# The first of three attention layers rewritten: 32-row score tiles, rows moved by DMA, and a step's projections, turns and output rows at its end

## The chip, the cores and the metric

The kernel runs on one core of one Trainium2 chip. The metric is the device time of one execution in microseconds (us). Three runs of the kernel before gave a median of 1830.98 us (1827.04 to 1831.57). The engines are named as in the profile: PE is TensorE, DVE is VectorE, ACT is ScalarE, POOL is GpSimd, SP is SyncE, which here only issues DMAs.

## The reference

Eight sequences of 256 rows and 160 channels pass through a small cross-attention layer, then through a transformer block of self-attention, cross-attention and a gated feed-forward. All of it is in FP32. Only the first layer is touched:

```python
residual = x                                   # (8, 256, 160)
text, ip = ctx[:, :77], ctx[:, 77:]            # of 512 context rows, 256 channels
q = split_heads(x @ Wq.T, 20)                  # 20 heads of 8 channels
out_text = attend(q, text @ Wk.T,   text @ Wv.T,   1 / sqrt(8))
out_ip   = attend(q, ip @ Wk_ip.T,  ip @ Wv_ip.T,  1 / sqrt(8))
x = (out_text + out_ip) @ Wo.T + bo + residual
# then, untouched: x += self_attention(norm(x)); x += cross_attention(norm(x), ctx); x += gated_ff(norm(x))
```

Each head has two softmaxes over the same queries, one over the 77 text keys and one over the 435 others, with a maximum and a sum of its own.

## The kernel before

Each layer is a function with a program for each engine, written out by hand; semaphores tie them together. FP32 precision on PE's fast FP32R format comes from splitting an operand into a high part (its rounded value) and a low part (the rest) and adding the products high x high, high x low and low x high.

`narrow_attention_layer` is the first layer. Its unit is a step, one group of 4 heads of one batch: 5 groups times 8 batches make 40 steps. A group's 4 heads take 32 rows each of the 128 partitions. These 32 rows are the head's 8 channels four times over: the weights are given with every column repeated four times, so that the projections themselves (`project`, L1281) put the channels on all four places. Marks by row (`q_signed`, `q4`, `k_signed`, `k4`; L1422, L1423, L1427, L1507 to L1521) then leave the high or the low part on each place, and the matmul over 32 rows adds the split products up. `masked_q` (L1409) writes a copy of q for each head, with the other heads' rows zero, so that a score matmul runs over all 128 rows and yields one head's scores.

A step has five stages that run in neighbouring steps, so that PE has work of several groups at hand: projections of group t; scores of t-1 (`score`, L1262), one head and 128 queries at a time into a double-buffered tile, whose negated maxima over text and other keys DVE takes (`maximum`, L1485); the maxima are turned by a transpose (L1363) and ACT places them as two extra rows of the masked q (L1439); turned scores of t-2, keys down and queries across (`turned_scores`, L1274), which then come out with the maximum already taken off, and which ACT exponentiates (`exp`, L1402); weighted sums of t-3 (L1322), where v has extra columns of ones, so that the denominators come out as rows of the same result; and for t-4 the `pick` matmul (L1356), which repeats the denominators on the rows of the sums, two reciprocals (L1494) and a product (L1532). In each group of five steps stand V's projection (L1376) and the output rows (L1345, added to x at L1516).

PE's order inside a step is written in `step`: eight slots, each with a score, a part of the projections or of the weighted sums, and turned scores. Ten steps, two batches, make a turn; of the four turns the first and the last are written out, and a hardware loop runs the middle two. SP loads the weights, then x and ctx of each batch, single-buffered. POOL does nothing in the loop.

## Time and profile before

| | us |
|---|---|
| median of 3 runs | 1830.98 |
| the profiled execution | 1826.65 |
| its span | 1824.9 |
| PE busy in the span | 1669.2 (91%) |
| DVE busy | 1163.7 (64%) |
| ACT busy | 951.1 (52%) |
| POOL busy | 346.0 (19%) |
| granted TensorE clock, mean | 0.971 |

The busy times are those of all four layers. The first layer runs from the start to about 533 us. The matmuls are pipelined, and their ends are modelled, so where PE is back to back the distance between two starts is what an instruction costs, not its duration. The granted clock is a share of 2.4 GHz; it has two levels, 1.2 and 2.4 GHz, and a value between them is a mean over a stretch.

### The profile page before, as it was taken

The numbers are of one execution on the slowest core, as the hardware profiler recorded it, in microseconds if no ns is written. First come the engines' busy times: TensorE is split into PE (matmuls) and PEld (weight loads), VectorE is DVE, ScalarE is ACT, GpSimd is POOL, SyncE is SP. The second block draws the span as 40 slices with busy tenths as digits, with TensorE's granted clock in tenths as the row PEclk, the third lists the DMA queues.
The fourth block names the chain that finished last, engine by engine and source line by source line (L and its number), as shares of the span: only waits on it lengthen the run. The fifth ranks groups of instructions, "written<-read, shape, count | busy, mean of one in ns | idle before, by whom it ended". The sixth has DMA issues, their size and how long they took to land. (4 is left out here: it accounts for less than half of the span.)

```text
span 1824.9 us, 43431 instructions
## 1 busy us (share of the span) xinstructions
PE 1669.2 (91%) x18560; PEld 1334.9 (73%) x18560; DVE 1163.7 (64%) x1934; ACT 951.1 (52%) x1634; POOL 346.0 (19%) x254
## 2 busy tenths in 40 slices
PE   5999989999967999999975999999999999999768
PEld 3677666667636888888864787878888887878558
DVE  5777767887757677677644565656565656554366
ACT  5778767887754444555424544444444444443233
POOL 1000000000003222222211332323232323222200
PEclk9999989999978999999997999999999999999979
DMA  5000000000002000000002000000101010000010
GB/s 214 18 19 1 18 20 1 18 19 1 1 23 80 2 2 2 2 2 2 2 1 68 25 2 25 1 25 2 24 2 25 2 25 2 1 2 2 2 45 22
DMA packets 13675, 34.21 MB, mean 19 GB/s; under 512 B 2033, under 2 KB 5105, under 8 KB 13105
## 3 DMA queue, kind: packets, MB, share of 16 engines
q1 hardware_dynamic: 13488, 31.47, 5.5%
q8 instruction: 149, 2.44, 0.6%
q14 instruction: 38, 0.30, 0.1%
HBM read 30.15 MB, written 1.31 MB: 17 GB/s over the span
## 5 line engine op out<-in xcount | busy, mean ns | idle before, releaser
L1485 DVE TENSOR_REDUCE l_negmax<-l_pscore 128x1 f32<-128x77 f32 (+1 forms) x640 | 233.2, 413 | 74.1 <-PE l_pscore L1262 69.5
L1046 DVE TENSOR_REDUCE a_negmax<-a_pscore 128x2 f32<-128x1024 f32 x160 | 195.6, 1223 | 115.5 <-PE a_pscore L821 115.5
L973 ACT ACTIVATE raw_weights<-a_pst 128x1024 f32<-128x1024 f32 x160 | 164.0, 1025 | 162.3 <-PE a_pst L846 161.6
L1402 ACT ACTIVATE l_probs<-l_pst 128x512 f32<-128x512 f32 x320 | 184.4, 598 | 75.1 <-PE l_pst L1274 74.2
L1119 POOL TENSOR_TENSOR raw_weights<-raw_weights 128x512 f32<-128x512 f32 x80 | 106.7, 1337 | 342.5 <-ACT raw_weights L973 342.5
L1262 PE MATMUL l_pscore<-l_k,l_qm 128*128 128x512 f32 x320 | 147.2, 460 | 11.5 <-DVE l_negmax L1485 6.0
L692 POOL TENSOR_TENSOR a_key_sum<-a_probs 128x1024 f32<-128x1024 f32 x40 | 96.2, 2405 | 240.8 <-ACT a_probs L568 240.8
L870 PE MATMUL a_pj<-a_ct,a_wk 64*128 64x512 f32 x960 | 130.3, 403 | 4.8 <-DVE a_ql L1034 3.8
L1274 PE MATMUL l_pst<-l_qm,l_k 128*128 128x256 f32 x640 | 131.0, 287 | 4.0 <-ACT l_probs L1402 3.3
L625 DVE TENSOR_REDUCE a_negmax<-a_pscore 128x4 f32<-128x1024 f32 x80 | 97.7, 1221 | 57.9 <-PE a_pscore L445 57.9
L880 PE MATMUL a_pj<-a_wv,a_ct 128*128 128x256 f32 x960 | 128.6, 291 | 4.1 <-DVE a_kl L1034 4.1
L1274 PEld LDWEIGHTS l_pst<-l_qm,l_k 128*128 128x128 f32 x640 | 116.0, 192 | 21.9 <-issue 5.0
L880 PEld LDWEIGHTS a_pj<-a_wv,a_ct 128*128 128x128 f32 x960 | 121.3, 194 | 4.8 <-issue 3.9
L1119 POOL TENSOR_TENSOR a_key_sum<-raw_weights 128x512 f32<-128x512 f32 x80 | 102.6, 1285 | 100.9 <-ACT raw_weights L973 100.9
L1060 DVE RECIPROCAL a_recip<-a_pv 128x256 f32<-128x256 f32 x40 | 70.3, 1758 | 78.7 <-PE a_pv L903 78.7
L870 PEld LDWEIGHTS a_pj<-a_ct,a_wk 64*128 64x128 f32 x960 | 87.5, 187 | 26.0 <-DVE a_ql L1034 7.8
L1322 PE MATMUL l_pv<-l_probs,l_v 128*32 128x256 f32 x1280 | 102.7, 394 | 0.5 <-ACT l_sums L1445 0.5
L256 POOL MEMSET a_ln_half<- 128x2 f32 x2 | 0.2, 100 | 542.9 <-POOLq L1158 528.1
L637 DVE RECIPROCAL a_recip<-a_pv 128x256 f32<-128x256 f32 x40 | 70.3, 1757 | 49.5 <-PE a_pv L508 49.5
L568 ACT ACTIVATE a_probs<-a_pst 128x1024 f32<-128x1024 f32 x80 | 81.9, 1023 | 37.8 <-PE a_pst L468 37.8
L840 PE MATMUL a_pst<-a_qh,a_kh 64*128 64x256 f32 x640 | 95.5, 292 | 6.3 <-ACT raw_weights L973 5.6
L1262 PEld LDWEIGHTS l_pscore<-l_k,l_qm 128*128 128x128 f32 x320 | 60.8, 190 | 48.1 <-issue 38.9
(186 smaller groups left out, 3840.5 us busy)
## 6 DMA issues: line engine op xcount, KB each, us to landing
l_ct<-in_ctx_t SPq DMA_DIRECT2D x8, 512.0 KB, 3.7
a_ct<-in_ctx_t SPq DMA_DIRECT2D x8, 512.0 KB, 5.0
a_ct<-in_ctx_t SPq DMA_DIRECT2D x16, 256.0 KB, 5.8
l_x<-in_x_t SPq DMA_DIRECT2D x8, 256.0 KB, 2.7
raw_weights<-in_a_wq SPq DMA_DIRECT2D x2, 960.0 KB, 4.9
raw_weights<-in_a_wv SPq DMA_DIRECT2D x1, 1920.0 KB, 11.3
a_wo<-in_a_wo SPq DMA_DIRECT2D x2, 800.0 KB, 6.4
xs<-in_x SPq DMA_DIRECT2D x8, 160.0 KB, 4.0
```

The source lines that it names most:

```text
L625: nc.vector.tensor_reduce(to, pscore[:].rearrange("p h (q k) -> p h q k", q=QT), AX.X, ALU.max, negate=True).then_inc(max_done, 1)
L692: nc.gpsimd.tensor_tensor(key_sum[:, e % 2], probs[:, e % 2, :, 0, :], probs[:, e % 2, :, 1, :], ALU.add).then_inc(sum_ready, 1)
L870: last = mm(pj[:, t, :], wk[OWN[t], hw, s, u * P:(u + 1) * P], cts[b % 2][OWN[t], hc, s, :], start=k == 0, stop=k == len(C_ROWS) - 1)
L880: last = mm(pj[:, kt // 2, (kt % 2) * STEP_COLS:(kt % 2 + 1) * STEP_COLS], cts[b % 2][:, hc, 2 * s, kt * P:(kt + 1) * P], wv[:, hw, s, u * ...
L973: nc.scalar.activation(probs[:, 2 * i:2 * i + 2, 2 * n:2 * n + 2, :], pst[:].rearrange("p h (k q) -> p h k q", k=2), ACT.Exp, scale=SCALE) ...
L1046: nc.vector.tensor_reduce(to, pscore[:], AX.X, ALU.max, negate=True).then_inc(max_done, 1)
L1119: nc.gpsimd.tensor_tensor(key_sums[n][:, two], probs[:, two, 2 * n, :], probs[:, two, 2 * n + 1, :], ALU.add).then_inc(sum_ready, 1)
L1262: mm(pscore[:, i % 2, :], qm[:, buf, j, qt * P:(qt + 1) * P], k4[:, buf, :], start=True, stop=True).then_inc(score_ready, 1)
L1274: last = mm(pst[:, n % 2, i * SQ:(i + 1) * SQ], k4[:, buf, kt * P:(kt + 1) * P], qm[:, buf, j, :], start=True, stop=True)
L1322: last = mm(pv[j * ROWS:(j + 1) * ROWS, 0:SQ], v[:, vb, kt, GROUP * u3 + j, :], probs[:, par, j, kt, :], start=kt == 0, stop=kt == KT - 1)
L1402: nc.scalar.activation(probs[:, par, j, 2 * kb:2 * kb + 2, :], pst[:, n % 2, :].rearrange("p (k q) -> p k q", k=2), ACT.Exp, scale=SCALE). ...
L1485: last = nc.vector.tensor_reduce(negmax[:, par, qt, j, s:s + 1], pscore[:, i % 2, keys], AX.X, ALU.max, negate=True)
```

## The change

The first layer is written anew. The other layers, and the reference's arithmetic, are the same.

The projections are made once per batch for all heads, with plain weights: ip keys and text keys of 16 heads (128 columns), `rest` (the last 4 heads' keys of both kinds), q, and v in four key blocks. ACT copies each result twice (`take`), once rounded (hi) and once in full, and POOL subtracts (`low`). SP then moves rows by DMA (`stack`): for each group, channel c of a head's high or low part goes to row 4c + r of a stack of 128 rows, so that a head has 32 rows again: three places for the split products and a fourth for the maxima, against marks of ones among the keys. POOL rounds the stacks (`round_stack`).

Scores and turned scores use 32 rows per head, two heads at once on different row groups of the array, instead of masked copies of q over 128 rows. One score tile holds two heads and 128 queries and isn't double-buffered; DVE reduces two heads at once. The maxima come back by one addition on DVE (`place_max`). The denominators of a batch are moved by DMA to 40 rows, inverted at once (`invert`), and spread over the sums' rows by five matmuls per batch (`spread`). There is one PSUM bank for projections and turned maxima (`pj`) and one for sums, spread denominators and output rows (`px`). V's copies leave POOL's zeros where nothing stands.

In a step PE now has four slots, each with one score pair and its turned scores, the weighted sums in the first; everything else stands behind them: a projection, the turned maxima, a piece of finishing (`s0`, `s1`, `s2` or `out`), another projection. `PLAN` says which. The projections are for the next batch, so the program begins with five steps that have nothing else. There is no hardware loop; every step is written out.

```diff
-    TURNS = B // 2
+    T_LAG, V_LAG = 2, 3
     SCALE = float(D0) ** -0.5
-    total = GROUPS * B
-    WIDE = GROUPS * P
+    ALL = GROUPS * B
+    FIRST, LAST = -GROUPS, ALL + 8
+    K_ROLES, Q_ROLES = ("hi", "lo", "hi"), ("hi", "hi", "lo")
+    MOVES = [16 * (6 if u < GROUPS - 1 else 9) for u in range(GROUPS)]
...
+        PLAN = {0: ("ip", "text"), 1: ("rest", "q"), 2: (None, None), 3: ("v0", "v1"), 4: ("v2", "v3")}
+        def finished(t):
+            b, k = divmod(t - 2 * GROUPS + 1, GROUPS)
+            return (("s0", "s1", "s2", "out")[k], b) if k < 4 and 0 <= b < B else None
...
+            def stack(m, u):
+                sp.wait_ge(k_low if u < GROUPS - 1 else rest_low, m + 1)
+                sp.wait_ge(q_low, m + 1)
+                wait(sp, rounded, GROUPS * (m - 1) + u + 1)
+                main = u < GROUPS - 1
+                rows = slice(u * ROWS, (u + 1) * ROWS) if main else slice(0, ROWS)
...
+                    for keys, src in moves:
+                        sp.dma_start(k_stack[r:P:4, u, keys], src.bitcast(FP32)).then_inc(stacked[u], 16)
+                for r, half in enumerate(Q_ROLES):
+                    sp.dma_start(q_stack[r:P:4, u, :], q_n[half][rows, 0 if main else 1].bitcast(FP32)).then_inc(
+                        stacked[u], 16)
...
+                if u == 2 and b + 1 < B:
+                    for group in range(GROUPS):
+                        stack(b + 1, group)
...
+            def score(g, s):
+                m, u = divmod(g, GROUPS)
+                qt, pair = s // 2, s % 2
+                if s == 0:
+                    pe.wait_ge(rounded, g + 1)
+                wait(pe, max_done, 4 * g + s)
+                for h in range(2):
+                    rows = slice((2 * pair + h) * ROWS, (2 * pair + h + 1) * ROWS)
+                    last = mm(pscore[:, h, :], q4[rows, u, qt * P:(qt + 1) * P], k4[rows, u, :],
+                              start=True, stop=True)
+                last.then_inc(score_ready, 1)
...
+            def turned_scores(g, s):
+                m, u = divmod(g, GROUPS)
+                n, pair = s // 2, s % 2
+                if s == 0:
+                    pe.wait_ge(pj_read, pj_uses["turn", g] + 1)
+                wait(pe, exp_done, 4 * g + s - 1)
                 for i in range(2):
+                    kt = 2 * n + i
+                    for h in range(2):
+                        rows = slice((2 * pair + h) * ROWS, (2 * pair + h + 1) * ROWS)
+                        last = mm(psts[s % 2][:, h, i * SQ:(i + 1) * SQ], k4[rows, u, kt * P:(kt + 1) * P],
+                                  q4[rows, u, :], start=True, stop=True)
                 last.then_inc(st_ready, 1)
...
+            def project(what, m):
+                wait(pe, pj_read, pj_uses[what, m])
...
+                elif what in ("ip", "text", "rest"):
+                    cols, n = {"ip": (IP, SK), "text": (TXT, TEXT + 1), "rest": (RST, SK)}[what]
+                    for k, (hw, hc, s) in enumerate(C_TERMS):
+                        last = mm(pj[:, 0:n], wc[:, hw, s, cols], ct[:, hc, s, 0:n],
+                                  start=k == 0, stop=k == len(C_TERMS) - 1)
...
+            def weighted_sums(g):
+                m, u = divmod(g, GROUPS)
+                wait(pe, px_read, px_uses["sum", g])
+                pe.wait_ge(pj_read, pj_uses["v3", m] + 1)
+                pe.wait_ge(exp_done, 4 * (g + 1))
+                for kt in range(KT):
+                    for j in range(GROUP):
+                        last = mm(px[j * ROWS:(j + 1) * ROWS, 0:SQ], v[:, m % 2, kt, GROUP * u + j, :],
+                                  probs[:, g % 2, j, kt, :], start=kt == 0, stop=kt == KT - 1)
+                last.then_inc(px_ready, 1)
+            def turn_max(g):
+                wait(pe, pj_read, pj_uses["turn", g])
+                pe.wait_ge(max_done, 4 * g + 4)
+                if g == 0:
+                    pe.wait_ge(*first_in)
+                for qt in range(QT):
+                    last = nc.tensor.transpose(pj[:, qt * P:(qt + 1) * P], negmax[:, g % 2, qt, :], ident)
+                last.then_inc(pj_ready, 1)
...
+            def finish(what, b):
+                wait(pe, px_read, px_uses[what, b])
+                if what == "out":
+                    pe.wait_ge(px_read, px_uses["s2", b] + 1)
...
+                else:
+                    pe.wait_ge(recip_done, b + 1)
+                    if b == 0:
+                        pe.wait_ge(small_in, 64)
+                    k = int(what[1])
+                    for i, u in enumerate(range(2 * k, min(2 * k + 2, GROUPS))):
+                        last = mm(px[:, i * SQ:(i + 1) * SQ], spread[:, u, :], recip[:], start=True, stop=True)
+                last.then_inc(px_ready, 1)
...
+            def step(t):
+                for s in range(4):
+                    if here(t):
+                        score(t, s)
+                    if here(t - T_LAG):
+                        turned_scores(t - T_LAG, s)
+                    if s == 0 and here(t - V_LAG):
+                        weighted_sums(t - V_LAG)
+                if projected(t, 0):
+                    project(*projected(t, 0))
+                if here(t - 1):
+                    turn_max(t - 1)
+                if finished(t):
+                    finish(*finished(t))
+                if projected(t, 1):
+                    project(*projected(t, 1))
...
+            def take(what, m):
+                act.wait_ge(pj_ready, pj_uses[what, m] + 1)
...
+                if what[0] != "v":
+                    for hi, x, src in pairs:
+                        copy(hi, src)
+                        copy(x.bitcast(FP32), src).then_inc(pj_read, 1)
...
+            def maximum(g, s):
+                qt, pair = s // 2, s % 2
+                if s == 0 and g >= 2:
+                    dve.wait_ge(pj_ready, pj_uses["turn", g - 2] + 1)
+                dve.wait_ge(score_ready, 4 * g + s + 1)
+                to = negmax[:, g % 2, qt].rearrange("p (j d r) -> p j d r", d=D0, r=4)[:, 2 * pair:2 * pair + 2, :, 3]
+                for k, keys in enumerate((slice(0, TEXT), slice(TEXT, SK))):
+                    last = nc.vector.tensor_reduce(to[:, :, k], pscore[:, :, keys], AX.X, ALU.max, negate=True)
                 last.then_inc(max_done, 1)
...
+            def place_max(g):
+                dve.wait_ge(pj_ready, pj_uses["turn", g] + 1)
+                to = q4[:, g % GROUPS, :]
+                nc.vector.tensor_tensor(to, to.bitcast(FP32), pj[:, 0:SQ], ALU.add).then_inc(pj_read, 1)
+            def invert(b):
+                dve.wait_ge(den_in[b % 2], 16 * GROUPS * (b // 2 + 1))
+                if b:
+                    dve.wait_ge(px_ready, px_uses["s2", b - 1] + 1)
+                n = GROUPS * DENS
+                nc.vector.reciprocal(recip[0:n, :], den[:, b % 2, :]).then_inc(recip_done, 1)
...
+            def round_stack(g):
+                m, u = divmod(g, GROUPS)
+                if g == 0:
+                    pool.wait_ge(marks_placed, 16 * GROUPS)
+                pool.wait_ge(stacked[u], MOVES[u] * (m + 1))
+                wait(pool, st_ready, 4 * (g - GROUPS + 1))
+                nc.gpsimd.tensor_copy(k4[:, u, :], k_stack[:, u, :])
+                nc.gpsimd.tensor_copy(q4[:, u, :], q_stack[:, u, :]).then_inc(rounded, 1)
```

PE's order in a whole step of the steady part: first before (`l_pa`, `l_pb` hold projections, `l_pv` the sums; this is from the turned maxima to the middle of the ip projection of a step).

```order
L1363 MATMUL l_pb<-identity,l_negmax 128x128 x2
L1262 MATMUL l_pscore<-l_k,l_qm 128x512
L1281 MATMUL l_pa<-l_nt,l_wq 128x256 x4
L1274 MATMUL l_pst<-l_qm,l_k 128x256 x2
L1262 MATMUL l_pscore<-l_k,l_qm 128x512
L1281 MATMUL l_pa<-l_ct,l_wk 128x256 x6
L1274 MATMUL l_pst<-l_qm,l_k 128x256 x2
L1262 MATMUL l_pscore<-l_k,l_qm 128x512
L1281 MATMUL l_pb<-l_ct,l_wk_ip 128x512 x3
L1274 MATMUL l_pst<-l_qm,l_k 128x256 x2
L1262 MATMUL l_pscore<-l_k,l_qm 128x512
L1281 MATMUL l_pb<-l_ct,l_wk_ip 128x512 x3
```

Now, a whole step with u = 0 and the start of its end block (`l_px` holds the sums, `l_pj` the projection, then the turned maxima, `l_recip`<-`l_spread` the spread denominators).

```order
L1304 MATMUL l_pscore<-l_k,l_q 128x512 x2
L1319 MATMUL l_pst<-l_q,l_k 128x256 x4
L1356 MATMUL l_px<-l_probs,l_v 32x256 x16
L1304 MATMUL l_pscore<-l_k,l_q 128x512 x2
L1319 MATMUL l_pst<-l_q,l_k 128x256 x4
L1304 MATMUL l_pscore<-l_k,l_q 128x512 x2
L1319 MATMUL l_pst<-l_q,l_k 128x256 x4
L1304 MATMUL l_pscore<-l_k,l_q 128x512 x2
L1319 MATMUL l_pst<-l_q,l_k 128x256 x4
L1338 MATMUL l_pj<-l_ct,l_wc 128x512 x6
L1367 MATMUL l_pj<-identity,l_negmax 128x128 x2
L1385 MATMUL l_px<-l_recip,l_spread 128x256 x2
```

Projections stood between scores and gave DVE time for its maxima; now only turned scores do, and the weighted sums once, and the projection and the turned maxima stand behind the last score.

ACT's order over most of a step, before (`l_qm` is the masked q):

```order
L1402 ACTIVATE l_probs<-l_pst 128x512 x2
L1422 ACTIVATE l_q_signed<-l_pa,l_marks 128x256
L1423 ACTIVATE l_k_signed<-l_pa,l_marks 128x77
L1402 ACTIVATE l_probs<-l_pst 128x512 x2
L1427 ACTIVATE l_k_signed<-l_pb,l_marks 128x435
L1409 ACTIVATE l_qm<-l_q,l_marks 128x256 x2
L1402 ACTIVATE l_probs<-l_pst 128x512
L1409 ACTIVATE l_qm<-l_q,l_marks 128x256 x2
L1402 ACTIVATE l_probs<-l_pst 128x512 x3
L1439 ACTIVATE l_qm<-l_pb 2x256 x4
```

and now, over a step with u = 0 (`l_k_hi`, `l_k_lo` are the two copies of a projection):

```order
L1426 ACTIVATE l_probs<-l_pst 128x2x512
L1412 ACTIVATE l_sums<-l_px 128x256
L1426 ACTIVATE l_probs<-l_pst 128x2x512 x3
L1412 ACTIVATE l_k_hi<-l_pj 128x435
L1412 ACTIVATE l_k_lo<-l_pj 128x435
L1412 ACTIVATE l_k_hi<-l_pj 128x77
L1412 ACTIVATE l_k_lo<-l_pj 128x77
L1426 ACTIVATE l_probs<-l_pst 128x2x512
L1412 ACTIVATE l_sums<-l_px 128x256
L1426 ACTIVATE l_probs<-l_pst 128x2x512 x3
```

The copies of q per head and the placing of maxima are gone, and the exps are half as many and twice as long; the projection's copies stand behind the last exp of the step, and the turned maxima on PE wait for them.

## Rows read from the trace of the kernel before

**Rows 1.** stage table, first layer; its first row names the columns

```profile
core 0: us, PE busy (x) PEld busy (x) DVE busy (x) ACT busy (x) POOL busy (x), PEclk, DMA share, GB/s
23.57:509.88 486.31, 453.76 (x3268) 331.15 (x3268) 373.95 (x909) 374.01 (x849) 0.00 (x0) 0.98 0.04 15
509.88:533.70 23.82, 16.85 (x108) 10.30 (x108) 8.71 (x13) 7.13 (x16) 0.00 (x0) 0.79 0.00 0
```

**Rows 2.** groups by line, first layer (count, busy us, mean ns)

```profile
L1485 DVE TENSOR_REDUCE l_negmax<-l_pscore 128x1 f32<-128x435 f32 x320 | 191.8, 599 | 0.0
L1402 ACT ACTIVATE l_probs<-l_pst 128x512 f32<-128x512 f32 x320 | 184.4, 598 | 75.1 <-PE l_pst L1274 74.2
...
L1485 DVE TENSOR_REDUCE l_negmax<-l_pscore 128x1 f32<-128x77 f32 x320 | 72.7, 227 | 74.1 <-PE l_pscore L1262 69.5 <-issue 4.2
L1409 ACT ACTIVATE l_qm<-l_q,l_marks 128x256 fp32r<-128x256 f32 x160 | 71.9, 504 | 0.0
...
L1439 ACT ACTIVATE l_qm<-l_pb 2x256 fp32r<-2x256 f32 x160 | 60.0, 375 | 26.4 <-PE l_pb L1363 23.4
```

**Rows 3.** timeline of PE, first layer: start, duration, instruction

```profile
46.48 1.04 PE L1376 MATMUL l_pb<-l_wv,l_ct 128*128 128x320 f32 x6
...
48.97 0.85 PE L1281 MATMUL l_pa<-l_ct,l_wk 128*128 128x256 f32 x6
...
50.12 0.86 PE L1281 MATMUL l_pb<-l_ct,l_wk_ip 128*128 128x512 f32 x3
50.82 0.40 PE L1274 MATMUL l_pst<-l_qm,l_k 128*128 128x256 f32 x2
...
53.68 0.40 PE L1274 MATMUL l_pst<-l_qm,l_k 128*128 128x256 f32 x2
54.01 0.64 PE L1322 MATMUL l_pv<-l_probs,l_v 128*32 128x256 f32 x8
54.58 0.49 PE L1262 MATMUL l_pscore<-l_k,l_qm 128*128 128x512 f32 x1
```

**Rows 4.** timeline of PE and DVE, third layer, tight score chain

```profile
1302.00 0.28 PE L840 MATMUL a_pst<-a_qh,a_kh 64*128 64x256 f32 x2
...
1302.12 0.29 PE L842 MATMUL a_pst<-a_qh,a_kl 64*128 64x256 f32 x2
...
1316.18 1.21 DVE L1046 TENSOR_REDUCE a_negmax<-a_pscore 128x2 f32<-128x1024 f32 x1
...
1317.44 0.50 PE L821 MATMUL a_pscore<-a_kh,a_qh 64*128 64x512 f32 x2 [0.51 <-DVE a_negmax L1046]
...
1317.99 1.23 DVE L1046 TENSOR_REDUCE a_negmax<-a_pscore 128x2 f32<-128x1024 f32 x1 [0.60 <-PE a_pscore L821]
```

**Rows 5.** groups by line and shape, whole run

```profile
L973 ACT ACTIVATE raw_weights<-a_pst 128x1024 f32<-128x1024 f32 x160 | 164.0, 1025 | 162.3 <-PE a_pst L846 161.6
...
L1532 DVE TENSOR_TENSOR l_ot<-l_sums,l_recip 128x256 f32<-128x256 f32 x40 | 17.0, 425 | 1.4
```

**Rows 6.** timeline of PE: the same output rows at either clock

```profile
492.04 2.88 PE L1345 MATMUL l_pd<-l_wo,l_ot 128*128 128x160 f32 x20
...
528.44 4.40 PE L1345 MATMUL l_pd<-l_wo,l_ot 128*128 128x160 f32 x20 [2.39 <-DVE l_ot L1532]
```

**Rows 7.** timeline of PE where the loop body starts again

```profile
255.00 0.79 PE L1262 MATMUL l_pscore<-l_k,l_qm 128*128 128x512 f32 x1 [3.57 <-issue]
```

**Rows 8.** stage table, PE alone: us, busy (x), clock, DMA share, GB/s

```profile
510.00:515.00 5.00, 2.75 (x12) 0.78 0.00 0
1712.00:1714.00 2.00, 0.88 (x16) 1.00 0.00 0
```

**Rows 9.** timeline of SP's queue and POOL at the start

```profile
1.20 4.40 POOL L1557 MEMSET l_v<- 128x2560 f32 x2
...
2.62 0.90 SPq L80 DMA_DIRECT2D raw_weights<-in_l_wk  x2
```

**Rows 10.** DMA issues by line: KB each, median us from issue to landing

```profile
l_x<-in_x_t SPq DMA_DIRECT2D x8, 256.0 KB, 2.7
```

More of the change, by code:

```diff
@@ new lines, in finished @@
+        def finished(t):
+            b, k = divmod(t - 2 * GROUPS + 1, GROUPS)
+            return (("s0", "s1", "s2", "out")[k], b) if k < 4 and 0 <= b < B else None
+        pj_uses, px_uses = {}, {}
+        for t in range(FIRST, LAST):
+            for use in (projected(t, 0), ("turn", t - 1) if here(t - 1) else None, projected(t, 1)):
+                if use:
+                    pj_uses[use] = len(pj_uses)
+            for use in (("sum", t - V_LAG) if here(t - V_LAG) else None, finished(t)):
+                if use:
+                    px_uses[use] = len(px_uses)
@@ L1461, in _, with copy, high_inputs @@
-            for part in range(3):
-                hi_inputs(0, part)
-            weights.high(act, pieces)
+            def copy(out, x, **kw):
+                return nc.scalar.activation(out, x, ACT.Copy, **kw)
+            def high_inputs(m):
+                act.wait_ge(ctx_in, 16 * (m + 1))
+                copy(cts[m % 2][:, 0], ct32[:]).then_inc(in_hi, 1)
+                act.wait_ge(x_in, 16 * (m + 1))
+                copy(nts[m % 2][:, 0], x32[:, 0])
+                copy(nts[m % 2][0:EXT, 2], x32[0:EXT, 1]).then_inc(in_hi, 1)
@@ new lines, in step @@
+            def step(t):
+                b, u = divmod(t, GROUPS)
+                for s in range(4):
+                    if here(t - T_LAG):
+                        exp(t - T_LAG, s)
+                    if s == 0 and here(t - V_LAG):
+                        copy_sums(t - V_LAG)
+                for place in range(2):
+                    if projected(t, place):
+                        take(*projected(t, place))
+                if u == 4 and b + 2 < B:
+                    high_inputs(b + 2)
@@ L1464, in _ @@
+            high_inputs(0)
+            act.wait_ge(wc_in, 16)
+            copy(wc[:, 0], raw_c).then_inc(w_hi, 1)
+            act.wait_ge(wq_in, 16)
+            copy(wq[:, 0], raw_q[:, 0])
+            copy(wq[0:EXT, 2], raw_q[0:EXT, 1]).then_inc(w_hi, 1)
             act.wait_ge(small_in, 64)
             act.wait_ge(v_marked, 1)
-            turns(act, step, 6)
+            for t in range(FIRST, LAST):
+                if t == -1:
+                    act.wait_ge(w_done, 3)
+                    load_next(act)
+                step(t)
@@ new lines, in step @@
+            def step(t):
+                b, u = divmod(t - 2 * GROUPS + 2, GROUPS)
+                for s in range(4):
+                    if here(t):
+                        maximum(t, s)
+                    if s == 1 and t >= 0 and t % GROUPS == 0 and t // GROUPS + 1 < B:
+                        low_rest(t // GROUPS + 1)
+                if here(t - 1):
+                    place_max(t - 1)
+                if finished(t):
+                    take(*finished(t))
+                if u == 0 and 0 <= b < B:
+                    invert(b)
@@ new lines, in _ @@
+            low_inputs(0)
+            for i in range(2):
+                nc.gpsimd.memset(v[:, i], 0.0)
+            nc.gpsimd.memset(negmax[:], 0.0)
+            nc.gpsimd.memset(recip[:], 0.0).then_inc(zeroed, 1)
+            for t in range(FIRST, LAST):
+                b, u = divmod(t, GROUPS)
+                for place in range(2):
+                    if projected(t, place) and projected(t, place)[0] in ("text", "rest", "q"):
+                        low(*projected(t, place))
+                if FIRST + 2 <= t < ALL - 3:
+                    round_stack(t + 3)
+                if u == 4 and b + 2 < B:
+                    low_inputs(b + 2)
+                if u == 0 and 0 <= b < B:
+                    if b == 0:
+                        pool.wait_ge(*first_in)
+                        pool.wait_ge(small_in, 64)
+                    nc.gpsimd.tensor_tensor(xs[:, b], xs[:, b], bo_rows[:], ALU.add).then_inc(biased, 1)
@@ new lines, in laid_out @@
+    wo = np.zeros((GROUPS, GROUP, 2, ROWS // 2, C), np.float32)
+    for u in range(GROUPS):
+        for s in range(2 * GROUP):
+            spread[2 * GROUP * u + s, u, s, 1:1 + D0] = 1
+    for k in range(2):
+        wo[:, :, k, 1:1 + D0] = w0["Wo"].reshape(GROUPS, GROUP, D0, C)
+    layers = {"l0": {"wq": wq, "wc": halves(wc).transpose(1, 0, 2), "wo": wo.reshape(GROUPS, P, C).transpose(1, 0, 2),
+                     "bo_rows": rows(inputs["L0_xattn_bo"]), "marks": marks,
+                     "spread": spread.reshape(P, GROUPS, P), "key_marks": key_marks.reshape(ROWS, SK)}}
```

541 lines of the change are left out of this document (200 added, 341 removed).

## The prediction

> **What bounds the kernel now.** I read the stage table first, then the groups by line, then the timelines. The first layer's scores begin at 23.57 and end at 509.88 us [rows 1]: 486.3 us for 40 steps, 12.2 us each, with PE busy 453.8 of them at a granted clock of 0.98. DVE is busy 374.0 and ACT 374.0, about 9.4 us a step each. So PE sets the step, with DVE and ACT close behind. The tail takes 23.8 us more at clock 0.79 [rows 1]. Inside one step PE goes back to back: three 512-column projections take 0.70 us from their start to that of the next instruction (50.12 to 50.82), six of 256 columns take 0.68 (48.97 to 49.65, where the six end their issue and their last one drains), two 256-column turned scores about 0.24, and one key block of the weighted sums with its two changes of tile shape 0.57 (54.01 to 54.58) [rows 3]. The rest of the program (two more attention layers and the feed-forward) isn't touched; it should move as a block.
>
> **What is computed less.** Of PE's work in a step, the 8 score matmuls of 512 columns and the 16 of 256 become 8 and 16 on 32 rows, issued in pairs on different row groups. The nearest rows are the pairs on 64 rows of the third layer: two matmuls of 256 columns start every 0.12 us (1302.00 to 1302.12) [rows 4]. So a pair of 512 costs 0.24, and a step's scores and turned scores cost 4 x 0.24 + 4 x 0.24 = 1.9 us instead of 8 x 0.24 + 8 x 0.24 = 3.8. That 32-row pairs go as 64-row pairs do is assumed: no row shows a 32-row tile. If they went one after the other, a step would have 1.9 us more. The projections are made once per batch for 20 heads, not once per group of four with every column repeated: per batch 12 matmuls of 512 columns, 8 of 256, 6 of 78, 6 of 320 and 18 of 160, by rows 3 about 2.8 + 0.9 + 0.5 + 0.9 + 1.5 = 6.6 us, against 5 x (0.45 + 0.68 + 1.40) + 3.5 = 16.2 before. DVE's 16 maxima of 599 and 227 ns (6.6 us) become 8 over two heads: the two sizes give 1.04 ns an element, so 154 elements take 0.31, 870 take 1.05, and the pair 1.29 (the 1024 elements of L1046 take 1.21 to 1.23, [rows 4]). ACT's four masked copies (504 ns) and four placements (375 ns) [rows 2] go; the eight exps of 598 ns become four of 1025 [rows 5]. The reciprocals fall to one per batch.
>
> **What is added: waits in a row.** The score tile isn't double-buffered any more: score s waits for maximum s-1. The third layer has this same chain: the reduce ends at 1317.39 (1316.18 + 1.21), the matmul starts at 1317.44, the next reduce at 1317.99, so DVE idles 0.60 in each turn [rows 4]. One turn costs 0.60 + 1.29 = 1.89 us. In a step: score 0, turned 0 and the weighted sums, now together, 0.24 + 0.24 + 0.1 + 4 x 0.45 + 0.15 = 2.5 (a key block of 0.57 without its changes of shape is about 0.45, which I take; with them the sum would be 2.9), which hides maximum 0; then two turns of 1.89; then score 3 and turned 3, 0.6. Together 6.9 us.
>
> Behind it stands the block at the step's end, all of it through one PSUM bank, pj, whose next use waits for its reader. ACT's last exp ends about 1.3 us into the block (turned 3 ready at about 0.25, 1.03 more). The five kinds of step:
> - u = 0: ip projection 1.5 until ready, two copies of 435 (under the 598 ns of 512 [rows 2]) 0.95, turn 0.2, the spread matmuls 0.9 beside DVE's addition of the turned maxima (0.43 [rows 5], 1.0 with both handshakes), text 0.45: 4.1
> - u = 1: rest 1.5, copies 1.1, turn and addition 1.0, q 0.85: 4.45
> - u = 2: turn 0.2, output rows 20 at 0.136 (2.88 in all [rows 6]): 3.05
> - u = 3: v0 1.04 [rows 3], its copies until 2.1, turn and addition 1.0, v1 0.5: 3.6
> - u = 4: v2 0.9, its copy at 1.65, turn and spread 1.2, v3 0.5: 3.35
> They sum to 18.55. A batch costs 5 x 6.9 + 18.55 + 0.9 (low_rest on DVE between two maxima, the output row's addition ahead of the next maximum) = 54.0 us, a step 10.8; 40 steps 432. The first steps lack turned scores, sums and output rows (-7), the last five have no next batch to project (-10, since the score chain then sets them): 415.
>
> **Start and end.** Before, the first score stands at 23.57. Now ACT takes its first projection only once v is marked, which waits for POOL's memsets of v (4.40 for two, [rows 9]) behind its low parts of the first inputs: about 15 us. Four projections follow one by one with their copies, partly at the slow clock, about 2.5 us each (25), POOL's low part 1.3, six DMAs at 0.45 of issue [rows 9], about 2 of landing (2.7 for 256 KB [rows 10]), two roundings 1.6: first score at 32.7, 9 us later. After the last score's step come two steps of turned scores bound by exps (11), the sums (2), then denominators by DMA, reciprocal, three spreads and the output rows, about 17: 30 us against 23.8. The unrolled program loses the loop's restart, where PE waited 3.57 us for its instructions [rows 7]; that is within the old 486.3. POOL's roundings, the moved rows (33 DMAs a batch at 0.45 = 15 us of SP's time in 54) and the one DMA of denominators per step lie beside this with three steps of slack, and cost nothing unless the slack is used up.
> Sum at full clock: 32.7 + 415 + 30 = 478 against 533.7, a gain of 55 us.
>
> **The clock is the unknown.** PE was busy 93% of the steps before. Now, in the middle of each step, it is busy for about 0.6 us in every 1.89, and the block at the end has idle spans of 1 us. In the rows, a stretch with PE busy 0.88 of 2.00 us kept 1.00, one with 2.75 of 5 fell to 0.78, which is a part of it at 1.2 GHz instead of 2.4 [rows 8]. The new middle lies under both. What a fall costs: 20 output matmuls take 2.88 us at 2.4 GHz and 4.40 when most of them run at 1.2 [rows 6]. A step wholly at 1.2 GHz would pay its sums and its end block almost twice and each score a little, 2.3 + 0.9 + 2.15 = 5.4 us. Bounds: 0 (clock kept) and 40 x 5.4 = 215 us. I expect that the dense parts (sums, projections) bring it back each time, and take a fifth of the time as slow, between the row that kept its clock and the one that fell (0.78 means 0.44 of its time slow): 1.1 us a step, 43 us. So 478 + 43 = 521, 12 us less than before. The profiled execution took 1826.65 us (span 1824.9) and the median is 1830.98; the difference carries over, so 1831 - 12 = 1819.
>
> The Trainium skill, "TensorE: Matmul & The Clock Gate", section "A second HAM failure mode: psum-queue depth-cycling", tells of a kernel whose short idles between groups of matmuls make the clock swing between its two levels, so that it pays for each fall and each rise. By it the second rival below would be the case. The trace agrees as far as it goes: 0.98 in the dense steps and 0.79 in the tail [rows 1].
>
> **Rivals.**
> - The clock holds. For: 0.88 of 2.00 busy kept 1.00 [rows 8], and no idle span here is above 1.4 us. Against: the new middle is thinner. Time: 1831 - 55 = 1776.
> - The clock falls in nearly every step and needs its dense part to rise, so that 40% of the first layer is slow: 0.4 x 215 = 86, less 55: 1862, slower. The place is the weighted sums and the ip, rest and output matmuls that follow the thin middle; it decides from a slow share of a quarter (54 us) upwards.
> - The moved rows come late: a step waits for the roundings because SP issues 33 DMAs in a row behind the denominators. The slack of three steps (32 us) covers 15 us of issue plus 3; it would need an issue of over 0.9 us each. Then 8 times some 8 us: about 1883 with the forecast's clock.
> - The pairs on 32 rows don't overlap: 40 x 1.0 on the path (half of 1.9 lies beside the maxima): 1859.
>
> **How the numbers follow.** Forecast 0.45, clock holds 0.17, clock falls often 0.30, late rows 0.04, no overlap 0.04. What a measurement of this kernel can't tell from no change is 0.3%, 5.5 us. The forecast's own range is 1797 to 1840 (slow shares from a tenth to three tenths), of which two thirds lie under 1825.5 and a quarter above 1836.5. That gives faster 0.47, same 0.13, slower 0.40. The range for 8 in 10 is 1776 to 1862: it takes in the clock that holds, and reaches to the middle of the case where it falls often.
>
> **What would show it.** Right: first score near 33 us; DVE idle 0.6 before maxima 1 to 3; the score group's reduces near 1.05 and 0.31; steps of 11 to 12.5 us; the first layer ending near 521; granted clock 0.9 in it; the layers after it unchanged within 2 us. Wrong: a clock of 1.00 or under 0.85 in the steps, PE waiting for POOL's rounding, pairs of score matmuls 0.2 us apart, or a later layer that moves.

## The result, and the profile after

The changed kernel takes 1932.3 us (median of 4 runs, 1925.48 to 1938.95) against 1831.11 for the kernel before on the same chip: a ratio of 1.0558, 95% interval 1.0513 to 1.0602. The forecast was 1819 and the range ended at 1862, so it was wrong in its sign and outside its range. The profiled execution took 1938.95 us (span 1937.2), the longest of the four. Ratios in this document leave out executions more than 1.5% above the fastest of the same kernel; that concerns one run, with 9 extra matmuls.

The stage table of the changed kernel, with the columns of [rows 1]: the 40 steps, the tail of the first layer, then the other three layers.

```profile
36.30:603.00 566.70, 436.13 (x2721) 289.56 (x2722) 249.09 (x396) 213.80 (x298) 91.19 (x121) 0.66 0.12 34
603.00:640.20 37.20, 27.97 (x191) 18.08 (x190) 7.42 (x12) 9.49 (x12) 0.00 (x1) 0.75 0.01 2
640.20:1096.40 456.20, 402.21 (x5640) 338.98 (x5640) 303.33 (x351) 215.27 (x294) 120.01 (x64) 0.94 0.06 19
1096.40:1873.60 777.20, 740.86 (x9084) 599.63 (x9084) 423.60 (x498) 323.71 (x413) 216.74 (x177) 0.98 0.04 12
1873.60:1937.20 63.60, 57.25 (x444) 55.35 (x444) 45.51 (x145) 20.96 (x47) 4.15 (x6) 1.00 0.06 21
```

The first layer now ends at 640.20 instead of 533.70: 106.5 us of the 112.3 by which the span grew. DVE fell from 374.0 to 249.1 us of work and ACT from 374.0 to 213.8, as meant, but PE's 454 only to 436, although it has much less to do: the granted clock of the steps went from 0.98 [rows 1] to 0.66. A clock of 0.66 means that 2 x (1 - 0.66) = 0.68 of the time ran at 1.2 GHz.

The groups by line, of the changed kernel's whole run, that answer to [rows 2]:

```profile
L1304 PE MATMUL l_pscore<-l_k,l_q 32*128 32x512 f32 x320 | 102.9, 639 | 97.9 <-DVE l_negmax L1512 95.7 <-POOL l_q L1608 2.2
L1356 PE MATMUL l_px<-l_probs,l_v 128*32 128x256 f32 x1280 | 119.5, 539 | 1.3 <-ACT l_probs L1426 0.8 <-DVE l_ot L1542 0.4
```

and, for the 40 steps alone, DVE's maxima and ACT's exps:

```profile
L1512 DVE TENSOR_REDUCE l_negmax<-l_pscore 128x2 f32<-128x870 f32 x160 | 168.8, 1055 | 0.1
L1512 DVE TENSOR_REDUCE l_negmax<-l_pscore 128x2 f32<-128x154 f32 x160 | 51.1, 319 | 220.3 <-PE l_pscore L1304 219.7
L1426 ACT ACTIVATE l_probs<-l_pst 128x1024 f32<-128x1024 f32 x152 | 155.6, 1024 | 144.1 <-PE l_pst L1319 143.5
```

Every engine waits for another one: PE 96 us for DVE's maxima, DVE 220 us for PE's scores. PE waits for POOL's rounding of the stacks 2.2 us in all, so the moved rows are not late.

PE in one step of the changed kernel (start, duration, instruction), a step with v2 and v3, wholly at 1.2 GHz:

```profile
458.49 0.79 PE L1304 MATMUL l_pscore<-l_k,l_q 32*128 32x512 f32 x2
459.08 0.62 PE L1319 MATMUL l_pst<-l_q,l_k 32*128 32x256 f32 x4
459.64 3.64 PE L1356 MATMUL l_px<-l_probs,l_v 128*32 128x256 f32 x32
463.21 0.79 PE L1304 MATMUL l_pscore<-l_k,l_q 32*128 32x512 f32 x2
...
465.39 0.80 PE L1304 MATMUL l_pscore<-l_k,l_q 32*128 32x512 f32 x2 [0.96 <-DVE l_negmax L1512]
...
467.57 0.80 PE L1304 MATMUL l_pscore<-l_k,l_q 32*128 32x512 f32 x2 [0.96 <-DVE l_negmax L1512]
468.17 0.63 PE L1319 MATMUL l_pst<-l_q,l_k 32*128 32x256 f32 x4
468.73 1.57 PE L1344 MATMUL l_pj<-l_wc,l_ct 128*128 128x160 f32 x6
470.71 0.69 PE L1367 MATMUL l_pj<-identity,l_negmax 128*128 128x128 f32 x2 [0.42 <-ACT l_v L1412]
471.19 1.91 PE L1385 MATMUL l_px<-l_recip,l_spread 128*128 128x256 f32 x4
472.55 1.76 PE L1344 MATMUL l_pj<-l_wc,l_ct 128*128 128x160 f32 x6
474.24 0.79 PE L1304 MATMUL l_pscore<-l_k,l_q 32*128 32x512 f32 x2
```

The step takes 15.75 us. From score 0 to score 1, with the weighted sums between, are 4.72 us (458.49 to 463.21), and a turn is 2.18 (465.39 to 467.57). At 2.4 GHz a turn is 1.89, as forecast; the same lines earlier in the run:

```profile
380.67 0.50 PE L1304 MATMUL l_pscore<-l_k,l_q 32*128 32x512 f32 x2 [1.15 <-DVE l_negmax L1512]
381.01 0.39 PE L1319 MATMUL l_pst<-l_q,l_k 32*128 32x256 f32 x4
382.56 0.70 PE L1304 MATMUL l_pscore<-l_k,l_q 32*128 32x512 f32 x2 [1.16 <-DVE l_negmax L1512]
```

Where the clock falls can be read from the score pairs, which take 0.50 us at 2.4 GHz and 0.79 at 1.2. The next step of that stretch:

```profile
390.23 3.24 PE L1356 MATMUL l_px<-l_probs,l_v 128*32 128x256 f32 x32
393.39 0.50 PE L1304 MATMUL l_pscore<-l_k,l_q 32*128 32x512 f32 x2
...
395.28 0.50 PE L1304 MATMUL l_pscore<-l_k,l_q 32*128 32x512 f32 x2 [1.14 <-DVE l_negmax L1512]
...
397.16 0.79 PE L1304 MATMUL l_pscore<-l_k,l_q 32*128 32x512 f32 x2 [1.15 <-DVE l_negmax L1512]
...
398.31 1.57 PE L1344 MATMUL l_pj<-l_wc,l_ct 128*128 128x160 f32 x6
```

In 33 of the 40 steps the fourth score pair takes over 0.6 us, in 27 the first, but in only 13 and 8 the second and the third. So the weighted sums mostly do bring the clock back, but begin slow themselves; it then serves the thin middle, is gone again by the fourth score, and the block at the end runs at 1.2 GHz.

PE and POOL at the start of the changed kernel:

```profile
32.52 1.57 PE L1344 MATMUL l_pj<-l_wc,l_ct 128*128 128x160 f32 x6 [0.42 <-ACT l_v L1412]
36.30 0.79 PE L1304 MATMUL l_pscore<-l_k,l_q 32*128 32x512 f32 x2 [2.22 <-POOL l_q L1608]
...
48.77 2.90 PE L1338 MATMUL l_pj<-l_ct,l_wc 128*128 128x512 f32 x6 [5.13 <-POOL l_nt L1581]
...
53.51 0.50 PE L1304 MATMUL l_pscore<-l_k,l_q 32*128 32x512 f32 x2
```

```profile
35.30 0.61 POOL L1607 CAST l_k<-l_k_stack 128x512 fp32r<-128x512 f32 x1 [8.21 <-DMA l_q_stack<-l_q_lo]
...
43.44 0.61 POOL L1607 CAST l_k<-l_k_stack 128x512 fp32r<-128x512 f32 x1 [7.19 <-DMA l_q_stack<-l_q_lo]
...
45.60 2.34 POOL L1581 TENSOR_TENSOR l_ct<-l_ct 128x1024 fp32r<-128x1024 f32 x1
```

Step 0 takes 17.2 us, since POOL splits batch 1's inputs only behind roundings that wait for DMAs.

### The profile page after: what moved, and what is told of

It is laid out like the page before. It is cut to its first block and busy times, and to the rows that moved or that the text cites. A ratio compares the mean times of both kernels' runs of the same rounds, so it can differ in the third digit from the quotient of the medians.

```text
span 1937.2 us, 41189 instructions
## 1 busy us (share of the span) xinstructions
PE 1680.5 (87%) x18128; PEld 1314.0 (68%) x18128; DVE 1034.2 (53%) x1409; ACT 794.9 (41%) x1085; POOL 446.5 (23%) x384
## 5 line engine op out<-in xcount | busy, mean ns | idle before, releaser
L1512 DVE TENSOR_REDUCE l_negmax<-l_pscore 128x2 f32<-128x154 f32 x320 | 206.5, 687 | 220.5 <-PE l_pscore L1304 219.7
L1426 ACT ACTIVATE l_probs<-l_pst 128x1024 f32<-128x1024 f32 x160 | 163.3, 1024 | 146.7 <-PE l_pst L1319 146.1
L1304 PE MATMUL l_pscore<-l_k,l_q 32*128 32x512 f32 x320 | 102.9, 639 | 97.9 <-DVE l_negmax L1512 95.7
L1304 PEld LDWEIGHTS l_pscore<-l_k,l_q 32*128 32x128 f32 x320 | 37.5, 231 | 147.4 <-DVE l_negmax L1512 114.2
L1356 PE MATMUL l_px<-l_probs,l_v 128*32 128x256 f32 x1280 | 119.5, 539 | 1.3 <-ACT l_probs L1426 0.8
L844 PE MATMUL a_pst<-a_ql,a_kh 64*128 64x256 f32 x640 | 92.0, 282 | 0.0
L846 PE MATMUL a_pst<-a_neg_t,a_sel 64*128 64x256 f32 x640 | 92.0, 282 | 0.0
L842 PE MATMUL a_pst<-a_qh,a_kl 64*128 64x256 f32 x640 | 91.7, 281 | 0.0
```

The source lines that it names most:

```text
L1304: last = mm(pscore[:, h, :], q4[rows, u, qt * P:(qt + 1) * P], k4[rows, u, :], start=True, stop=True)
L1356: last = mm(px[j * ROWS:(j + 1) * ROWS, 0:SQ], v[:, m % 2, kt, GROUP * u + j, :], probs[:, g % 2, j, kt, :], start=kt == 0, stop=kt == KT - 1)
L1426: nc.scalar.activation(probs[:, g % 2, 2 * pair:2 * pair + 2, 2 * n:2 * n + 2, :], psts[s % 2][:].rearrange("p h (k q) -> p h k q", k=2), ...
L1512: last = nc.vector.tensor_reduce(to[:, :, k], pscore[:, :, keys], AX.X, ALU.max, negate=True)
```

## The experiments

Theory: the change's own sum at full clock is right, and the slow clock is the loss. Rival: the serial chain (single score tile, one bank, everything at the step's end) is the loss, and the clock only accompanies it. All ratios are to the kernel before, whose own is 1.

**Work added to PE beside the maxima.** Runs with 6 and with 2 extra matmuls in slots 1 to 3, 6 on 32 rows, and 6 on 32 columns:

```diff
+            def fill():
+
+                for i in range(6):
+                    mm(px[:, SQ:SQ + 256], wc[0:128, 0, 0, 0:P], wc[0:128, 0, 0, 0:256], start=True, stop=True)
+
...
+                    if s in (1, 2, 3) and here(t):
+                        if here(t - V_LAG):
+                            pe.wait_ge(px_read, px_uses["sum", t - V_LAG] + 1)
+                        fill()
```

The run with 2 has `range(2)`, the one on 32 rows `wc[0:32, ...]` in both operands, the one on 32 columns `px[0:ROWS, ...]` and `wc[..., 0:ROWS]`.

> The changed kernel with 6 extra matmuls of 128 rows and 256 columns (fp32r) behind the turned scores of slots 1, 2 and 3 of each step, into the unused half of the bank of the sums; their result is not used. They add 3 x 0.64 us of PE work a step at full clock, and nothing to the chain while it stands at full clock. Theory (the slow clock is the loss: 0.69 of the 40 steps' time was at 1.2 GHz, and a step wholly slow pays about 5.4 us): the granted clock of the first layer rises above 0.9, steps come to 10.5 to 11.5 us, the first layer ends near 500 instead of 640, time 1785 to 1820. Rival (the serial chain, maxima and one bank for projections, is the loss, and the low clock only accompanies the idle time): steps stay at 14 us or get longer, time 1930 or more.

> The same with 2 extra matmuls in each of slots 1 to 3, a third of the amount (0.64 us a step at full clock). Theory (slow clock is the loss): the slow share falls from 0.69 but not to nothing, and the time follows it at 5.4 us for a step wholly slow: between 1800 and 1920, on a line with the changed kernel and the run with 6. Rival (serial chain): 1930 to 1945.

> As the run with 6, but each extra matmul uses 32 rows of the array instead of 128, for the same time on PE. If the clock goes by the time in which PE streams, this gives what the run with 128 rows gives (within 15 us). If it goes by how many rows of the array work (the score pairs on 32 rows would then count little), the clock stays near 0.65 in the first layer and the time stays above 1900.

> As the run with 6 extra matmuls of 128 rows, but each uses only 32 of the array's columns (output rows) instead of 128; time on PE and rows of the array are as there. If the clock goes by the rows that work, time as with 128 x 128: 1820 to 1840. If it goes by rows times columns, this is as thin as the run on 32 rows: 1885 to 1910. If neither counts but the time alone, the run on 32 rows has no explanation.

| extra work | us | ratio, 95% | clock of the steps |
|---|---|---|---|
| none | 1932.3 | 1.0558 [1.0513, 1.0602] | 0.66 |
| 6, 128 rows x 128 columns | 1827.8 | 0.9983 [0.9973, 0.9992] | 0.97 |
| 2, 128 x 128 | 1895.1 | 1.0373 [1.0324, 1.0422] | 0.74 |
| 6, 32 rows x 128 columns | 1897.8 | 1.0365 [1.0341, 1.0389] | 0.73 |
| 6, 128 rows x 32 columns | 1823.7 | 0.9964 [0.9951, 0.9976] | 0.97 |

Adding useless work wins 104 us. The stage rows of the steps in these four runs, first with 6 of 128 x 128:

```profile
36.27:500.00 463.73, 407.85 (x3444) 296.88 (x3444) 250.12 (x397) 213.83 (x298) 91.39 (x121) 0.97 0.14 41
```

With 2 of 128 x 128:

```profile
33.37:561.00 527.63, 435.31 (x2960) 297.32 (x2961) 249.82 (x396) 213.47 (x298) 91.20 (x121) 0.74 0.13 36
```

With 6 of 32 rows x 128 columns:

```profile
34.43:568.00 533.57, 466.22 (x3441) 339.53 (x3442) 249.79 (x396) 213.36 (x298) 91.17 (x121) 0.73 0.12 36
```

With 6 of 128 rows x 32 columns:

```profile
36.34:498.00 461.66, 399.27 (x3448) 274.68 (x3448) 250.43 (x398) 213.32 (x298) 91.35 (x121) 0.97 0.14 42
```

Stage rows of the run with 6 of 128 x 128, five steps (one batch) and the step of the kind that was shown slow above:

```profile
222.14:280.08 57.94, 51.46 (x462) 38.12 (x462) 32.14 (x52) 28.83 (x41) 12.42 (x16) 1.00 0.14 41
269.20:280.08 10.88, 9.97 (x94) 7.53 (x94) 6.73 (x11) 5.15 (x7) 0.96 (x2) 1.00 0.09 23
```

That slow step in the changed kernel:

```profile
458.49:474.24 15.75, 13.41 (x76) 9.08 (x76) 6.38 (x11) 5.14 (x7) 0.96 (x2) 0.50 0.03 8
```

The extra work of the last slot stands on the path. A later run that has none there (9 in slots 1 and 2) has the same steps at 11.60, 11.98 and 10.11 us instead of 12.21, 12.62 and 10.81, so it costs 0.65. Without it a batch takes 57.94 - 5 x 0.65 = 54.7, where the forecast had 54.0. And the slow step pays 15.75 - (10.88 - 0.65) = 5.5 us, where the forecast had 5.4. The 0.65 is measured on three kinds of step and taken for all five. At 1827.8 us the run with 6 missed its own range of 1785 to 1820 by 8 us, far from the rival's 1930: the 0.65 in each of 40 steps, 26 us, was reckoned as nothing. So the theory stands for the gap between forecast and result, and the rival falls for it; what the block at the end costs at full clock was in the forecast, and is measured below. The run with 2 lies between, as expected.

The extra work on 32 rows came out between what its two theories gave (not within 15 us of the first run, not quite above 1900), but far nearer to "rows count": PE is busy 0.87 of the steps in it (466.22 of 533.57) and 0.88 in the run with 128 rows, yet the clock is 0.73 and 0.97; 32 columns with all rows hold 0.97. PE's time is not quite equal, though: in slot 3 the extra matmuls on 32 rows start beside the score pair on other rows (at 201.67 and 201.65), and at full clock PE then idles 0.34 and 0.45 us before scores 2 and 3, where the run with 128 rows has 0.25. That this little time makes the difference is unlikely beside the run with 2: PE is busy only 0.83 of the steps there, and the clock is the same (0.74). PE's timeline of the run on 32 rows shows it streaming when the clock falls: gaps of 0.3 us at most, and then a score pair of 0.79 us instead of 0.50:

```profile
224.73 0.97 PE L1391 MATMUL l_px<-l_wc 32*128 32x256 f32 x6
225.99 0.50 PE L1304 MATMUL l_pscore<-l_k,l_q 32*128 32x512 f32 x2 [0.29 <-DVE l_negmax L1521]
226.32 0.40 PE L1319 MATMUL l_pst<-l_q,l_k 32*128 32x256 f32 x4
226.56 1.16 PE L1391 MATMUL l_px<-l_wc 32*128 32x256 f32 x6
227.87 0.79 PE L1304 MATMUL l_pscore<-l_k,l_q 32*128 32x512 f32 x2 [0.15 <-DVE l_negmax L1521]
```

So idle time is hardly all. That the changed kernel's own scores (pairs of 32 rows where 128 stood) let the clock fall in the same way follows from this by analogy; it wasn't tried on them alone.

**The start alone.** The next layer's weights are asked for in step 8 instead of -1, and batch 1's inputs split ahead of the roundings:

```diff
-                if t == -1:
+                if t == 8:
                     act.wait_ge(w_done, 3)
                     load_next(act)
...
-                if u == 4 and b + 2 < B:
+                if u == (2 if b < 0 else 4) and b + 2 < B:
                     high_inputs(b + 2)
...
+                if b < 0 and u == 2:
+                    low_inputs(1)
                 if FIRST + 2 <= t < ALL - 3:
                     round_stack(t + 3)
...
```

> The changed kernel with another start only: the next layer's three weight DMAs are issued in step 8 instead of step -1 (where they share the DMA engines with the first stacks of moved rows), and batch 1's inputs are split on ACT and POOL in step -3, ahead of the roundings, instead of behind them. In the changed kernel the last DMA of stack 0 was issued at 30.87 and its reader on POOL began at 35.30, that of stack 1 took 8 us, and PE waited 5.1 us for POOL in step 0. Theory (contention and POOL's order at the start cost about 10 us): first score at 33 to 34, step 0 at 11 to 13 us instead of 17.2, time 1918 to 1926. Rival (the moved rows are late because SP issues 33 DMAs at 0.6 us each): first score and step 0 within 1 us of before, time 1928 to 1938.

1918.5 us, 1.0501 [1.0473, 1.0528]. The first score is at 33.85, and step 0 takes 11.97 us instead of 17.2; its stage row in this run:

```profile
33.85:45.82 11.97, 6.76 (x21) 3.71 (x21) 5.58 (x9) 1.28 (x3) 1.92 (x4) 1.00 0.27 69
```

The first score may be chance: it stands at 33.37 to 36.34 us in the five other runs whose start was left alone. Step 0 is not: it takes 16.9 to 19.8 us in those, and 12.0 to 13.4 in all six with the new start. The median fell by 13.8 us, by the two ratios by about 10, and their intervals just overlap; what lies beyond step 0 is steps at another clock later (0.67 over the steps), as it also differs between executions (1914.32 to 1927.22). Of the two edits, that of the weights is seen in the DMAs: the stack's DMAs of 64 KB land in 2.1 us between 25 and 50 us here, where the changed kernel had 5.9. How much of step 0 each edit won was not taken apart.

**The end block spread over the slots.** This undoes one part of the change and adds no work (PE's part; the readers on ACT and DVE move with it):

```diff
                     if s == 0 and here(t - V_LAG):
                         weighted_sums(t - V_LAG)
-                if projected(t, 0):
+                    if s == 1 and projected(t, 0):
                         project(*projected(t, 0))
-                if here(t - 1):
+                    if s == 2 and here(t - 1):
                         turn_max(t - 1)
-                if finished(t):
+                    if s == 2 and finished(t):
                         finish(*finished(t))
-                if projected(t, 1):
+                    if s == 3 and projected(t, 1):
                         project(*projected(t, 1))
```

> Undoes one part of the change: the work that stands together at a step's end is spread over the slots (first projection behind slot 1, turned maxima and finishing behind slot 2, second projection behind slot 3; the readers on ACT and DVE in the same slots). No work is added. Theory (thin middle of the step lowers the clock, and the end block stands on the path): the matmuls of the end block fill PE's idle time beside the maxima; step 2.3 + 1.9 + 2.3 + 1.9 + 0.6 = 9.0 us at full clock, slow share under 0.3, first layer 430 to 480, time 1730 to 1790. Rival (ACT's and DVE's readers of the one bank, now between the exps and maxima, delay the chain as much as before): steps 12 to 14 us, time 1870 to 1930.

> The spread version with the same new start. In the spread version step 0 took 19.8 us. Theory (start costs 10 us there too): 1752 to 1762, first layer ending near 457 to 465. Rival (the clock, slow at the start in either case, takes it back): 1764 to 1770.

> The spread version with the new start and extra matmuls of 128 rows and 256 columns where a slot is thin: 2 ahead of a projection, 6 where a step has none, 3 ahead of the finishing matmuls (none with the output rows). Spread fast steps were 8.5 to 10.2 us, 9.2 on average, and 0.29 of the steps' time was slow. Theory (the rest of the loss is again the clock): slow share under 0.1, time 1725 to 1745. Rival (the extra work is on PE's path in the slots with projections): steps 0.3 to 0.6 us longer at full clock, time as without it or up to 10 us more.

Spread: 1768.5 us, 0.9655 [0.9634, 0.9676]. With the new start: 1753.5, 0.9581 [0.9565, 0.9597]. With extra matmuls in its thin slots: 1734.2, 0.9482 [0.9466, 0.9498]. The stage row of the steps, spread alone:

```profile
35.04:437.60 402.56, 329.85 (x2728) 217.52 (x2728) 244.72 (x397) 210.07 (x298) 91.31 (x121) 0.85 0.16 47
```

Spread with the new start:

```profile
34.36:429.00 394.64, 329.83 (x2729) 218.74 (x2728) 244.79 (x397) 210.19 (x299) 88.36 (x119) 0.87 0.18 53
```

Spread with the new start and extra matmuls:

```profile
31.01:407.00 375.99, 344.31 (x3083) 245.45 (x3082) 245.17 (x398) 212.69 (x299) 88.37 (x119) 0.96 0.19 55
```

One batch of the second of them at full clock takes 45.8 us, 8.9 less than 54.7; its stage row:

```profile
237.28:283.11 45.83, 38.97 (x372) 26.96 (x372) 31.37 (x52) 28.23 (x43) 12.41 (x16) 1.00 0.19 51
```

So the block at the end cost 1.8 us a step even at full clock, 71 us in 40. The steps of the spread version take 164 us less than the changed kernel's (402.6 for 566.7): the other 93, by subtraction, came with the clock, 0.66 to 0.85. The rival of the first of these runs falls. That of the third was right in one half, since its batch at full clock grew from 45.8 to 47.5, 0.33 us a step, and wrong in the other: the time went down by 19 us.

**The change's own order with the clock held.** New start, 9 extra matmuls in slots 1 and 2 only:

> The changed kernel in its own order (everything else at the step's end), with the new start and 9 extra matmuls of 128 rows in slots 1 and 2 only, where they lie beside a maximum and not on the path. This is the closest to the forecast's sum at full clock: 33 to the first score, 54.0 us a batch, tail 30, first layer 478. The run with 6 had 57.9 us a batch at full clock, of which 5 x 0.64 was its last slot's extra work. Theory (that sum is right and only the clock was mis-sized): fast batches 54 to 55.5 us, first layer ending at 490 to 505, time 1787 to 1802. Rival (the step's end block costs more than I reckoned, extra work apart): batches stay near 57, time 1812 or more.

1822.6 us is the median; but the four executions lie between 1798.87 us (mean clock 0.963) and 1834.2 (0.941). The ratio is 0.9865 [0.9815, 0.9915]. In the profiled execution (1834.2) the clock still fell in most steps with v2 and v3. The other four steps of a batch in it, as a stage row:

```profile
405.49:450.49 45.00, 41.39 (x370) 31.00 (x370) 25.85 (x42) 23.65 (x34) 11.45 (x14) 0.99 0.11 29
```

With 10.23 for the missing kind a batch is 55.2, within the theory's 54 to 55.5, and not the rival's 57. The fastest execution lies within the theory's 1787 to 1802; the median lies where the rival's time did (1812 or more), but by the clock and not by a longer batch: this order keeps its clock in one execution and not in the next, and why is open.

**Towards a best version.** The sums split over slots 0 and 1 and the output rows over slots 2 and 3, first in every step, then the sums only where slot 1 has no projection (this is the second, the sums alone):

```diff
-                        weighted_sums(t - V_LAG)
+                        weighted_sums(t - V_LAG, range(0, KT - (projected(t, 0) is None)))
+                    if s == 1 and here(t - V_LAG) and projected(t, 0) is None:
+                        weighted_sums(t - V_LAG, range(KT - 1, KT))
```

> The spread version with the new start and extra matmuls, with three edits: the last quarter of the weighted sums moves from slot 0 to slot 1, the output rows are made half in slot 2 and half in slot 3, and extra matmuls also stand in steps 0 to 2. In the version before it score 1 came 2.5 us after score 0 (the sums of 1.93 us over it) where a turn takes 1.89, and the step with output rows had 3.7 us from score 2 to score 3. Theory (PE's work in single slots sets the step): 2.5 us a batch from the sums and 1.4 from the output rows, 25 to 30 us in all, 5 more at the start: 1700 to 1712. Rival (the turns of 1.89 and DVE's additions take their place): 1722 to 1735.

> As the run before last (spread, new start, extra matmuls), with the sums split only in steps that have no first projection (one in five, and the last five), the output rows half in slot 2 and half in slot 3, and no extra matmuls in steps 0 to 2. In the run that split the sums in every step the fast steps were 10.65, 9.62, 8.84, 8.51 and 9.22 us (46.8 a batch) against 10.64, 9.47, 10.15, 8.36 and 8.81 (47.4) without a split: the step without projections won 1.3, and three others gave 0.7 back, since the moved quarter stood ahead of their projection. Theory (only a slot with room takes work): 46.1 a batch, 1.3 x 8 = 10 us less than 1734: 1720 to 1727. Rival (the split steps in a row change the clock or the denominators' way): 1731 to 1737.

In every step: 1736.0, 0.9484 [0.946, 0.9507]: no gain over the version without a split, against the expectation. A batch took 46.84 us instead of 47.46, and steps 0 to 2 took 35.2 instead of 31.4. A batch with the split:

```profile
176.78:223.62 46.84, 43.89 (x404) 30.55 (x405) 31.64 (x52) 28.09 (x42) 12.40 (x16) 1.00 0.18 51
```

and without:

```profile
172.97:220.43 47.46, 44.19 (x412) 31.87 (x412) 31.38 (x52) 28.64 (x42) 12.40 (x16) 1.00 0.18 50
```

Only where there is room: 1729.5 us, 0.9443 [0.9421, 0.9465], 5.6% faster than the kernel before, and the fastest here, though the interval only just clears that of the version without a split ([0.9466, 0.9498]); 2.5 us above what was expected. A batch took the 46.1 us that were expected, but the first score came 2.7 us later (33.71 for 31.01) and steps 0 to 4 took 52.4 us instead of 50.2, in a part that the edit hardly touches.

## Why the prediction was wrong

The step that failed is the clock term: "I expect that the dense parts (sums, projections) bring it back each time, and take a fifth of the time as slow". The slow share was 0.68. Put into the forecast's own terms, 0.68 x 215 = 146 us instead of 43, the sum is 1831 - 55 + 146 = 1922, against 1932 measured. That it comes so near is partly luck: 215 us is a price for 40 steps, and 0.68 is a share of time. The 385 us at 1.2 GHz would be 24.5 steps of 15.75, which at 5.5 cost 135; but by the score pairs above its slow time lay mostly in the dense parts, which pay most. Step by step:

- Wrong, and the whole of the sign: the slow share. The second rival had the place and mechanism right (falls in nearly every step, deciding from a share of a quarter) at a chance of 0.30, but stopped at 40%. "Bring it back each time" was not false but too late: by the score pairs the clock was back behind the sums in most steps and gone again in 33 of 40 at the fourth score, so that the dense parts themselves ran slow. I took my fifth from between the two stretches of [rows 8], both of which were busy on more rows of the array than a 32-row pair is. The runs with extra work speak for rows and not time alone, and no row of before could show it.
- Right: the price of a slow step (5.4; measured 5.5), the batch at full clock (54.0; 54.7), the turn (1.89), the reduces (1.05 and 0.31; 1.055 and 0.319), pairs on 32 rows that overlap. A score pair takes 0.34 until the next instruction where I had 0.24; it lies beside the maximum.
- Start, wrong by 3.6 us (36.30 for 32.7; 0.7 to 3.6 over the runs with this start) and another 5 in step 0: the stack's DMAs shared the DMA engines with the next layer's weights, and POOL split batch 1's inputs behind the roundings. I priced the DMAs one by one at an idle queue, and POOL's order not at all. Issuing one took 0.59 us on SP, too, and not 0.45.
- Tail, 37.2 for 30, at clock 0.75, where the old one had 0.79 [rows 1]. No experiment took the tail apart.
- "The layers after it unchanged within 2 us": they take 1297.0 us instead of 1291.2, with the same number of matmuls and PE busy 6 us longer. In the other runs they took 1290 to 1296 us. That it is where the clock happens to fall in them is likely and not shown.
- The late rows rival: PE waited 2.2 us for roundings; out. No overlap of pairs: out. "The clock holds" gave 1776; the nearest made, 9 extra matmuls and the new start, reached 1798.87 at best.

The range failed because its upper end was the middle of a rival whose own bound was 1831 - 55 + 215 = 1991. The chances didn't follow from their parts either: 0.45 / 4 + 0.30 + 0.04 + 0.04 is 0.49 for slower and leaves 0.04 for same, where I wrote 0.40 and 0.13.

## What to carry to other kernels

When a change takes work from a dense engine and puts waits in a row in its place, price it at both clock levels and give the slow one the larger chance unless each stretch stays about as dense as one that kept its clock; less work can cost more time. Put what stands in a block at the end of a step beside the waits in the middle: here that was worth 1.8 us a step at full clock, and more than that again through the clock. Where an idle slot can't be filled with real work, extra matmuls on all rows are worth a trial: they took 104 us off here.

## What the hardware showed that I had not expected

- With PE busy for nearly the same share of the steps (0.87 and 0.88), extra matmuls on 32 rows of the array left the clock at 0.73, those on 128 rows at 0.97; using 32 or 128 columns made no difference to it (0.97 in both).
- The clock column is not to be trusted before its first change: step 0 of the changed kernel is shown at 1.00, yet its score pairs take 0.79 us, as at 1.2 GHz, not 0.50. With these 15 us the slow share of the steps is about 0.71 instead of 0.68.
- A DMA of a stack took 2.1 us to land in the median of the run, and 5.9 beside the loads of the next layer's weights; with these loads moved away it took 2.1 in the same stretch. DMA issues between 25 and 50 us of the changed kernel (KB each, median us to landing):

```profile
raw_weights<-in_a_wv ACTq DMA_DIRECT2D x1, 1920.0 KB, 12.1
...
l_k_stack<-l_k_hi SPq DMA_DIRECT2D x8, 64.0 KB, 5.9
```
